# Second attention of a two-block gated cross-attention network: another order of the steps on TensorE

## The chip, the cores and the metric

The kernel runs on one core of a Trainium2 chip. The metric is the device time of one execution in microseconds, as the median of several runs.

## What is computed

The network takes 32 sequences of 128 tokens with 128 channels (x) and a context of 77 tokens with 128 channels for each sequence. It has two blocks. Each is a gated attention to the context, then a gated feed-forward that sends every token to one of eight experts. The part that matters here is the second block:

```
x = x + tanh(g_xattn[0]) * attention_0(layernorm(x), ctx)            # one head
x = x + tanh(g_ffn[0])   * experts_0(layernorm(x))                   # 8 experts and a shared one
x = x + tanh(g_xattn[1]) * attention_1(layernorm(x), ctx)            # 16 heads of 8, relative bias, no mask set
x = x + tanh(g_ffn[1])   * experts_1(layernorm(x))

def attention_1(q, ctx):
    scores = q_heads @ k_heads.T * scale + rel_bias                  # 16 heads, 128 x 77 each
    return (softmax(scores) @ v_heads).merge_heads() @ Wo + bo

def experts_1(x):                                                    # 8 maps of 128 x 128
    idx = argmax(x @ sign(tile_sigs).T)
    return (x @ W[idx] + b[idx])
```

All arithmetic on TensorE is in float32.

## The kernel before

The kernel works through stages: the first attention, the first feed-forward, and then one loop (`attend_1`) that does the second attention and the second feed-forward together, one sequence (batch) at a time. The change lies in this loop. Its first transpose on TensorE starts at 229.9 us, and it ends with the span.

Each engine has its own list of steps with a lag. `pipeline` goes through turns; in turn i it runs, in the order of the list, each step for batch i minus the step's lag. A turn thus holds steps of several batches side by side, and the order of the list is the order in which the engine issues. An engine that waits holds all that stands behind it in its list. There are 32 batches and the largest lag on TensorE is 5, so it takes 37 turns. In the first turns, parts of the first feed-forward's shared expert are mixed in (`shared`).

These are the steps on TensorE, by the line of their matmul:

- `norm_T` (L1267, lag 0), `queries` (L1271, lag 1): the normed input is transposed and projected.
- `scores(0)`, `scores(1)` (L1281 and L1285): scores of eight heads each, in products that use 32 rows of the array. VectorE adds the relative bias behind them (`bias`, L1482).
- `probs_T(0)` to `probs_T(3)` (L1295): the 16 heads' scores are kept in ten blocks of 128 columns, which are transposed 4, 1, 4 and 1 at a time. Those of the first half are already exponentials. Those of the second half come from VectorE's subtraction of the maximum (L1499); ScalarE takes the exponential when it copies them out of PSUM. The copies on ScalarE (L1400) are 512 and 128 columns wide.
- `weigh(0)` to `weigh(3)` (L1309): products of these with the values, eight matmul instructions each, for four outputs of 32 columns of the array. weigh(n) waits for ScalarE's copy of probs_T(n). weigh(0) and weigh(1) give the first half, weigh(2) and weigh(3) the second.
- `heads_T` (L1321), `mixed_T` (L1326), `project` (L1330, lag 4): the outputs are transposed, divided by the sums on VectorE (`mix`), transposed and projected. VectorE adds the residual (`residual`, L1520 to L1525).
- `norm3_T` (L1337, lag 4), `signature` (L1341, lag 5), `choice_T` (L1354, lag 5), `maps(0)` and `maps(1)` (L1349, lag 5), `picked_bias` (L1358, lag 5): the feed-forward. All of them write PSUM bank 7, one after another. VectorE stands between them: `choose` (L1532 to L1539) after the signature, `pick(0)` (L1550) after maps(0), `pick(1)` (L1553) after maps(1), `add_bias` (L1559) after picked_bias. ScalarE copies norm3_T's result (L1428) and choice_T's (L1433).

ScalarE's list has the copies in this order: norm3_T, probs_T(1), mixed_T, norm_T, probs_T(2), choice_T, probs_T(3), then the eight exponentials of the first half (L1390), the heads' copy (L1418) and the queries' (L1383).

VectorE's list is: choose, bias(0), maxima(0), residual, pick(0), bias(1), stats2 (L1470, L1473), pick(1), maxima(1), add_bias, mix, subtract.

Of the kernel before, what the change touches and what calls it, by code (L numbers as in the profile page):

```python
# [135 lines left out]
def wait(eng, sem, value):  # L136

    if isinstance(value, int) and value <= 0:
        return
    eng.wait_ge(sem, value)  # L140
# [8 lines left out]
def pipeline(eng, n, stages, ways=2, begin=None):  # L149

    first = min(lag for _, lag in stages)
    stages = [(stage, lag - first) for stage, lag in stages]
    span = max(lag for _, lag in stages)
    turns = -(-(n + span) // ways)

    for i in range(turns):
        if begin:
            begin(i)  # L160
        for u in range(ways):
            for stage, lag in stages:
                item = ways * i + u - lag
                if 0 <= item < n:
                    stage(item, (u - lag) % ways)
# [1019 lines left out]
def attend_1(nc, sb, sem, sems, bank, out, m, f, units):  # L1185
# [64 lines left out]
    def pe_program(pe):  # L1250
# [3 lines left out]
        def shared(place):  # L1254
            def stage(b, u):
                for n in range(*(PE_SHARED.get((place, b), (0, 0)) if isinstance(b, int) else (0, 0))):
                    j, part = piece(n)
                    if part < HC:
                        units["gate_up"](pe, EARLY + j, part)
                    else:  # L1260
                        units["down"](pe, EARLY + j)
            return stage
# [10 lines left out]
        def scores(half):  # L1273
            def stage(b, u):
                if half == 0:
                    pe.wait_ge(s["qs"], b + 1)
                    pe.wait_ge(s["kb"], b + 1)
                wait(pe, s["sb"], NHF * b + half)
                for i in two:
                    rows = slice(32 * (2 * half + i), 32 * (2 * half + i) + 32)  # L1280
                    nc.tensor.matmul(bS[i][:, 0:HG * SK], onesb[rows, :],  # L1281
                                     padR[rows, b:b + 1, :].to_broadcast([32, HG, SK]), start=True, stop=False)
                for i in two:
                    rows = slice(32 * (2 * half + i), 32 * (2 * half + i) + 32)
                    nc.tensor.matmul(bS[i][:, 0:HG * SK], QT[u][rows, :], KB[u][rows, :, :],  # L1285
                                     start=False, stop=True).then_inc(s["sc"], 1)
            return stage

        def probs_T(n):
            def stage(b, u):  # L1290
                half, end = divmod(n, 2)
                pe.wait_ge(s["su" if half else "ex"], b + 1)
                wait(pe, s["pTs"], N * b + n - 1)
                for i, c in enumerate(range(half * BH + end * HG, half * BH + (BH if end else HG))):
                    last = nc.tensor.transpose(bP[end][:, i * 128:i * 128 + 128], SB[u][:, c, :], ident)  # L1295
                last.then_inc(s["pT"], 1)
            return stage

        def weigh(n):
            def stage(b, u):  # L1300
                half, end = divmod(n, 2)
                pe.wait_ge(s["pTs"], N * b + n + 1)
                if n == 0:
                    pe.wait_ge(s["vp"], b + 1)
                    wait(pe, s["os"], b)
                    if isinstance(b, int) and b == 0:
                        pe.wait_ge(h["prod"], 2 * (EARLY + LATER) - 1)
                for j in range(HG):
                    last = nc.tensor.matmul(bO[32 * j:32 * j + 32, half * S:half * S + S],  # L1309
                                            VP[u][:, half, j, end, :, :].rearrange("p t r -> p (t r)"),  # L1310
                                            PT[half][:, (j + end) * S:(j + end) * S + S], start=(end == 0), stop=(end == 1))
                last.then_inc(s["pv"], 1)
            return stage
# [29 lines left out]
        def maps(k):  # L1343
            def stage(b, u):
                if k == 0:
                    pe.wait_ge(s["hTs"], b + 1)
                else:
                    pe.wait_ge(s["pk"], 2 * b + 1)
                nc.tensor.matmul(bF[:, :], xn3T[u][:, :], w2[:, k * HT:(k + 1) * HT, :], start=True, stop=True).then_inc(s["f"], 1)  # L1349
            return stage  # L1350
# [5 lines left out]
        def picked_bias(b, u):  # L1356
# [1 line left out]
            nc.tensor.matmul(bF[:, 0:128], OHT[u][:, :], b2[:, :], start=True, stop=True).then_inc(s["fb"], 1)  # L1358

        pipeline(pe, B, [  # L1360
            (signature, 5), (weigh(0), 3), (probs_T(2), 3), (weigh(1), 3), (probs_T(3), 3), (choice_T, 5),
            (project, 4), (weigh(2), 3), (maps(0), 5), (scores(1), 2), (weigh(3), 3), (maps(1), 5),
            (shared("queries"), 0), (queries, 1), (shared("T0"), 0), (probs_T(0), 2), (heads_T, 3),
            (picked_bias, 5), (shared("sc01"), 0), (scores(0), 1), (norm3_T, 4), (probs_T(1), 2),
            (mixed_T, 3), (shared("norm_T"), 0), (norm_T, 0)])
# [329 lines left out]
```

## Time and profile before

| | |
|---|---|
| median of 3 runs | 538.32 us (538.27 to 540.05) |
| the profiled execution, its own time | 539.62 us |
| its span | 537.8 us |
| TensorE matmul busy over the span | 484.3 us (90%) |
| VectorE | 383.5 us (71%) |
| ScalarE | 311.1 us (58%) |
| GpSimd | 353.2 us (66%) |

The span runs from the first to the last instruction on the chip; the time has a little more around it. A busy share is a mean over stages with different limits, and a matmul's record includes the time until the array is through with it, so that records overlap. In the profile's rows PE is TensorE, PEld its weight loads, DVE VectorE, ACT ScalarE and POOL GpSimd.

### The profile page before, as it was taken

To read this page: it belongs to the slowest core of one execution; us is meant where nothing else is said; L and a number is where in the kernel's file an instruction comes from. 1 tells how busy PE (TensorE), PEld (TensorE's weight loads), DVE (VectorE), ACT (ScalarE), POOL (GpSimd) and SP (SyncE) were. 2 spreads that over 40 slices of the span, in tenths; PEclk is the share of its full clock that TensorE was granted. 3 is DMA by queue.
4 is the path that set the end of the run, shared out by engine and by line. 5 is a ranking of instruction groups with operands and counts; after the bars stand their busy time and mean duration, and the time that the engine had idled before them with its cause. 6 is when DMAs were issued, how large, how long until landed. Compare 5 with 4: busy or idle time off the path is not lost.

```text
span 537.8 us, 12347 instructions
## 1 busy us (share of the span) xinstructions
PE 484.3 (90%) x3355; PEld 304.2 (57%) x3355; DVE 383.5 (71%) x1146; ACT 311.1 (58%) x1013; POOL 353.2 (66%) x845
## 2 busy tenths in 40 slices
PE   6868798589999999789999999999999999999863
PEld 5757687346655666565555556555555555556420
DVE  3778788548433434336999999999999999998631
ACT  3667687422245555258776766667666776766410
POOL 5574688877135555454778878788887878877421
PEclk9999897569999999959999999999999999999955
DMA  9855250022134322100000000000000000000000
GB/s 230 163 101 148 70 175 15 22 69 70 34 87 119 87 75 71 44 11 6 12 22 11 22 12 21 21 12 21 11 21 21 12 22 11 21 12 11 6 11 5
DMA packets 33924, 25.78 MB, mean 48 GB/s; under 512 B 8104, under 2 KB 31280, under 8 KB 33824
## 3 DMA queue, kind: packets, MB, share of 16 engines
q1 hardware_dynamic: 30864, 19.48, 14.6%
q0 software_dynamic: 2272, 4.67, 2.8%
q10 hardware_dynamic: 720, 0.83, 0.6%
q8 instruction: 29, 0.48, 0.4%
q14 instruction: 39, 0.32, 0.2%
HBM read 16.89 MB, written 8.39 MB: 47 GB/s over the span
## 4 chain that ended last, share of the span: by engine, by line
PE 47%; DVE 3%; issue 1%; POOL 0%; ACT 0%; POOLq 0%; DVEq 0%
PE bank L1349 13%; PE bank L1309 8%; PE bank L1295 8%; PE bank L1285 6%; PE bank L1358 2%; PE bank L1341 2%; PE bank L1281 1%; PE bank L1337 1%; PE bank L1326 1%; PE bank L1330 1%; PE bank L1271 1%; PE bank L1321 1%; PE bank L1354 1%; PE bank L1267 1%; DVE V L1550 1%
## 5 line engine op out<-in xcount | busy, mean ns | idle before, releaser
L1349 PE MATMUL bank<-w,xn3T 128*128 128x512 f32 x128 | 75.8, 676 | 2.4 <-DVE V L1550 2.0
L1390 ACT ACTIVATE wgu<-wgu,top 128x77 f32<-128x77 f32 x256 | 67.4, 347 | 15.5 <-DVE top L1492 15.5
L1400 ACT ACTIVATE PRT<-bank 128x512 f32<-128x512 f32 (+1 forms) x128 | 54.4, 426 | 29.5 <-PE bank L1295 29.5
L970 POOL DMA_INDIRECT routed<-ys,to x39 | 37.2, 953 | 48.1 <-DVE ys L1173 39.9
L1295 PE MATMUL bank<-cst,wgu 128*128 128x128 f32 x320 | 60.2, 286 | 0.4 <-ACT wgu L1390 0.2
L1482 DVE TENSOR_TENSOR wgu<-bank,biasQ 128x616 f32<-128x616 f32 x64 | 50.8, 794 | 8.6 <-PE bank L1285 7.0
L1309 PE MATMUL bank<-PRT,VP 128*32 128x128 f32 x1024 | 54.5, 285 | 0.7 <-ACT PRT L1400 0.7
L1492 DVE TENSOR_REDUCE top<-wgu 128x8 f32<-128x616 f32 x64 | 50.3, 785 | 1.1
L1285 PE MATMUL bank<-KB,QT 32*128 32x308 f32 x256 | 50.3, 434 | 0.0
L1625 POOL TENSOR_TENSOR wgu<-V 128x256 f32<-128x256 f32 x32 | 37.8, 1180 | 16.1 <-DVE V L1553 16.1
L1295 PEld LDWEIGHTS bank<-cst,wgu 128*128 128x128 f32 x320 | 37.8, 142 | 14.9 <-issue 13.4
L1168 DVE TENSOR_TENSOR hid<-actg,bank 128x256 f32<-128x256 f32 x39 | 16.4, 421 | 41.4 <-ACT actg L1077 41.4
L1026 PE MATMUL bank<-wgu,xsT 128*128 x78 | 40.7, 604 | 0.4 <-ACT xsT L1072 0.4
L833 POOL DMA_INDIRECT sorted_x<-XN,slot x32 | 33.3, 1040 | 8.5 <-issue 8.2
L1585 POOL TENSOR_TENSOR VP<-XN,cst 128x64 f32<-128x64 f32 x128 | 35.4, 308 | 0.0
L1309 PEld LDWEIGHTS bank<-PRT,VP 128*32 128x32 f32 x1024 | 20.1, 108 | 24.6 <-issue 19.1
L1604 POOL TENSOR_TENSOR x2b<-x,rows 128x128 f32<-128x128 f32 x32 | 14.5, 454 | 24.9 <-DVE x L1520 24.9
L1349 PEld LDWEIGHTS bank<-w,xn3T 128*128 128x128 f32 x128 | 19.9, 195 | 18.1 <-DVE V L1550 9.7
L1553 DVE COPY_PREDICATED V<-OH,bank 128x512 f32<-128x512 uint32 x32 | 23.5, 735 | 9.2 <-PE bank L1349 7.0
L1499 DVE TENSOR_TENSOR wgu<-wgu,top 128x616 f32<-128x616 f32 x32 | 27.0, 844 | 0.0
L1042 PE MATMUL bank<-wdn,hidT 128*128 x156 | 25.8, 288 | 1.1 <-ACT hidT L1082 1.1
L1077 ACT ACTIVATE actg<-bank 128x256 f32<-128x256 f32 x39 | 15.0, 384 | 20.2 <-PE bank L1026 20.2
(231 smaller groups left out, 1260.2 us busy)
## 6 DMA issues: line engine op xcount, KB each, us to landing
xs<-sorted_x SPq DMA_DIRECT2D x39, 64.5 KB, 1.8
wgu<-in_wgu SPq DMA_DIRECT2D x4, 512.0 KB
y<-routed SPq DMA_DIRECT2D x32, 64.0 KB, 1.8
out<-res SPq DMA_DIRECT2D x32, 64.0 KB, 1.7
ctxT<-in_ctxT SPq DMA_DIRECT2D x16, 77.0 KB, 3.2
mask<-in_mask SPq DMA_DIRECT2D x16, 77.0 KB, 3.9
wdn<-in_wdn SPq DMA_DIRECT2D x2, 512.0 KB
X<-in_x SPq DMA_DIRECT2D x1, 768.0 KB, 5.7
```

The source lines that it names most:

```text
L970: nc.gpsimd.indirect_dma_start(routed, bass.IndirectOffsetOnAxis(ap=to[:, t:t + 1], axis=0), ys[t % WAYS][:, :], None).then_inc(st_y[t % W ...
L1026: nc.tensor.matmul(bH[t % 2][:, :], xsT[t % 2][:, :], wgu[:, bass.ds(experts[t], 1), :], start=True, stop=True).then_inc(e["h"], 1)
L1285: nc.tensor.matmul(bS[i][:, 0:HG * SK], QT[u][rows, :], KB[u][rows, :, :], start=False, stop=True).then_inc(s["sc"], 1)
L1295: last = nc.tensor.transpose(bP[end][:, i * 128:i * 128 + 128], SB[u][:, c, :], ident)
L1309: last = nc.tensor.matmul(bO[32 * j:32 * j + 32, half * S:half * S + S], VP[u][:, half, j, end, :, :].rearrange("p t r -> p (t r)"), PT[ha ...
L1349: nc.tensor.matmul(bF[:, :], xn3T[u][:, :], w2[:, k * HT:(k + 1) * HT, :], start=True, stop=True).then_inc(s["f"], 1)
L1390: last = nc.scalar.activation(SC[u][:, head, :], SC[u][:, head, :], ACT.Exp, bias=top[u][:, head:head + 1])
L1400: nc.scalar.activation(PT[half][:, k], bP[end][:, 0:k.stop - k.start], ACT.Exp if half else ACT.Copy).then_inc(s["pTs"], 1)
L1482: nc.vector.tensor_tensor(half(SC[u][:, k, :]), bSS.rearrange("p c (h k) -> p c h k", h=HG), half(biasQ[:, k, :]), ALU.add).then_inc(s["sb ...
L1492: nc.vector.tensor_reduce(top[u][:, k], SC[u][:, k, :], AX.X, ALU.max, negate=(h == 0)).then_inc(s["mx" if h else "lo"], 1)
L1585: last = nc.gpsimd.tensor_tensor(VP[u][:, c, :, end, :, 0:HD], VF[:, first:first + HG, bass.ds(b, 1), :].to_broadcast([128, HG, 2, HD]), o ...
L1625: nc.gpsimd.tensor_tensor(sum2[u][:, :, :], picked[u][:, 0:2, :], picked[u][:, 2:4, :], ALU.add).then_inc(s["s2"], 1)
```

## The change

In the list of TensorE's steps, weigh(1) moves ahead of probs_T(2), project moves ahead of choice_T, and weigh(3) moves from behind scores(1) to directly behind weigh(2), ahead of maps(0). The lags stay, and so do the lists of all other engines.

```diff
         pipeline(pe, B, [
-            (signature, 5), (weigh(0), 3), (probs_T(2), 3), (weigh(1), 3), (probs_T(3), 3), (choice_T, 5),
-            (project, 4), (weigh(2), 3), (maps(0), 5), (scores(1), 2), (weigh(3), 3), (maps(1), 5),
+            (signature, 5), (weigh(0), 3), (weigh(1), 3), (probs_T(2), 3), (probs_T(3), 3), (project, 4),
+            (choice_T, 5), (weigh(2), 3), (weigh(3), 3), (maps(0), 5), (scores(1), 2), (maps(1), 5),
             (shared("queries"), 0), (queries, 1), (shared("T0"), 0), (probs_T(0), 2), (heads_T, 3),
             (picked_bias, 5), (shared("sc01"), 0), (scores(0), 1), (norm3_T, 4), (probs_T(1), 2),
             (mixed_T, 3), (shared("norm_T"), 0), (norm_T, 0)])
```

In the rows of the two programs a name on the right of the arrow is what is read: PRT and VP are the copied exponentials and the values, cst is the identity of a transpose, wgu the scores, OH the choice, AOT and wc the projection, xn3T and w (or w2) the maps. A float32 matmul is one row here and two records in the trace.

The first place is TensorE between the signature and the first maps of one turn, before:

```order
L1341 MATMUL bank<-wc,xn3T 128x8
L1309 MATMUL bank<-PRT,VP 32x128 x4
L1295 MATMUL bank<-cst,wgu 128x128 x4
L1309 MATMUL bank<-PRT,VP 32x128 x4
L1295 MATMUL bank<-cst,wgu 128x128
L1354 MATMUL bank<-cst,OH 8x128
L1330 MATMUL bank<-wc,AOT 128x128
L1309 MATMUL bank<-PRT,VP 32x128 x4
L1349 MATMUL bank<-w,xn3T 128x512
```

And the same place after:

```order
L1341 MATMUL bank<-wc,xn3T 128x8
L1309 MATMUL bank<-PRT,VP 32x128 x8
L1295 MATMUL bank<-cst,wgu 128x128 x5
L1330 MATMUL bank<-wc,AOT 128x128
L1354 MATMUL bank<-cst,OH 8x128
L1309 MATMUL bank<-PRT,VP 32x128 x8
L1349 MATMUL bank<-w,xn3T 128x512
```

Three blocks of four products with the values have become two of eight, and the second of them holds weigh(3), which stood behind the first maps.

The second place is TensorE from the first maps to the queries, before:

```order
L1349 MATMUL bank<-w,xn3T 128x512
L1281 MATMUL bank<-padR,onesb 128x308 x2
L1285 MATMUL bank<-KB,QT 128x308 x2
L1309 MATMUL bank<-PRT,VP 32x128 x4
L1349 MATMUL bank<-w,xn3T 128x512
L1271 MATMUL bank<-xn2T,wc 128x128
```

And after:

```order
L1349 MATMUL bank<-w,xn3T 128x512
L1281 MATMUL bank<-padR,onesb 128x308 x2
L1285 MATMUL bank<-KB,QT 128x308 x2
L1349 MATMUL bank<-w,xn3T 128x512
L1271 MATMUL bank<-xn2T,wc 128x128
```

The products of weigh(3) no longer stand between scores(1) and the second maps.

## Rows read from the trace of the kernel before

**Rows 1.** Three stretches: start:end, length; busy and count by engine; granted clock; DMA.

```profile
440.00:460.00 20.00, 20.00 (x171) 11.39 (x169) 18.47 (x44) 14.19 (x50) 16.05 (x45) 1.00 0.07 21
495.40:503.80 8.40, 7.69 (x64) 4.17 (x64) 7.23 (x18) 5.03 (x18) 3.68 (x9) 1.00 0.03 8
511.80:521.80 10.00, 6.54 (x13) 2.49 (x12) 3.31 (x10) 1.31 (x4) 2.85 (x8) 0.57 0.02 7
```

**Rows 2.** TensorE in order of time, one turn: start us, us, line, tiles.

```profile
444.61 0.39 PE L1341 MATMUL bank<-wc,xn3T 128*128 128x8 f32 x2
444.93 0.43 PE L1309 MATMUL bank<-PRT,VP 128*32 128x128 f32 x8
445.29 0.66 PE L1295 MATMUL bank<-cst,wgu 128*128 128x128 f32 x4
...
446.23 0.33 PE L1295 MATMUL bank<-cst,wgu 128*128 128x128 f32 x1
446.40 0.27 PE L1354 MATMUL bank<-cst,OH 128*8 128x128 f32 x1
446.50 0.39 PE L1330 MATMUL bank<-wc,AOT 128*128 128x128 f32 x2
446.82 0.43 PE L1309 MATMUL bank<-PRT,VP 128*32 128x128 f32 x8
447.18 1.12 PE L1349 MATMUL bank<-w,xn3T 128*128 128x512 f32 x2
...
448.99 0.43 PE L1309 MATMUL bank<-PRT,VP 128*32 128x128 f32 x8
449.35 1.13 PE L1349 MATMUL bank<-w,xn3T 128*128 128x512 f32 x2
...
451.31 0.37 PE L1358 MATMUL bank<-b,OHT 8*128 8x128 f32 x1
...
453.07 0.39 PE L1341 MATMUL bank<-wc,xn3T 128*128 128x8 f32 x2
```

**Rows 3.** Line L1341 over the span: ns min/median/max, first and last start.

```profile
L1341 PE MATMUL bank<-wc,xn3T x64: 256/275/381, 258.1 to 522.1; 128*128 128x8 f32 x64
```

**Rows 4.** VectorE in order of time, in the same turn.

```profile
445.70 0.40 DVE L1539 TENSOR_SCALAR OH<-am 128x8 f32<-128x8 f32 x1
...
448.25 0.18 DVE L1525 BATCH_NORM_AGGREGATE mv<-st 128x2 f32<-128x6 f32 x1
448.38 0.69 DVE L1550 TENSOR_TENSOR V<-bank,OH 128x512 f32<-128x512 f32 x1
...
450.24 0.18 DVE L1473 BATCH_NORM_AGGREGATE mv<-st 128x2 f32<-128x6 f32 x1
450.51 0.74 DVE L1553 COPY_PREDICATED V<-OH,bank 128x512 f32<-128x512 uint32 x1
...
451.84 0.35 DVE L1559 SCALAR_TENSOR_TENSOR x3b<-bank,dead,x 128x128 f32<-128x128 f32 x1
```

**Rows 5.** ScalarE in order of time, in the same turn and just before.

```profile
443.02 0.58 ACT L1400 ACTIVATE PRT<-bank 128x512 f32<-128x512 f32 x1
443.50 0.48 ACT L1406 ACTIVATE xn<-x,nb,r 128x128 f32<-128x128 f32 x1
...
445.98 0.60 ACT L1400 ACTIVATE PRT<-bank 128x512 f32<-128x512 f32 x1 [0.91 <-PE bank L1295]
446.70 0.27 ACT L1433 ACTIVATE OHT<-bank 8x128 f32<-8x128 f32 x1
446.88 0.25 ACT L1400 ACTIVATE PRT<-bank 128x128 f32<-128x128 f32 x1
```

**Rows 6.** TensorE in narrow windows: the halves of one block of products.

```profile
444.93 0.32 PE L1309 MATMUL bank<-PRT,VP 128*32 128x128 f32 x4
...
445.06 0.29 PE L1309 MATMUL bank<-PRT,VP 128*32 128x128 f32 x4
```

**Rows 7.** TensorE in the last turns: a pair of maps records.

```profile
513.93 2.08 PE L1349 MATMUL bank<-w,xn3T 128*128 128x512 f32 x2
```

## Prediction

> **What bounds the kernel now.** I read the busy times first, then the table of stretches, then the order of time of one turn on TensorE, ScalarE and VectorE. In the second attention TensorE is shown busy for all of 20 us in the stretch from 440 to 460 us, VectorE for 18.5 of them, ScalarE for 14.2 and GpSimd for 16.1, at the full clock (1.00, the 2.4 GHz level) [rows 1]. A busy TensorE is not proof that it sets the pace: its records overlap and a matmul that drains counts as busy. So I followed one turn, from the signature product at 444.61 to the next one at 453.07, which is 8.46 us [rows 2]. The 32 signatures lie between 258.1 and 522.1 us [rows 3], 8.5 apart in the mean (264.0 / 31), so this turn stands for the stage.
>
> A chain through one PSUM bank (bank 7) closes on itself once in a turn: signature, choice on VectorE, choice_T on TensorE, its copy on ScalarE, first maps, first pick on VectorE, second maps, second pick, picked bias, its addition on VectorE, third norm's transpose and its copy, and the next signature. The links that I use: the choice ends at 446.10 and choice_T starts at 446.40, though an engine's end reaches a waiting TensorE product in 0.06 (second pick ends 450.51 + 0.74 = 451.25, picked bias starts 451.31) [rows 2, 4]. The copy of the choice ends at 446.97 and the first maps start at 447.18, 0.21 later, because the third product block (weigh(2)) stands between [rows 2, 5]. The first pick ends at 449.07 and the second maps start at 449.35, 0.28 later, because weigh(3) stands between [rows 2, 4]. So TensorE's order has slack in the chain at three places. VectorE is close behind: its first pick starts 0.05 before the previous operation's end (448.25 + 0.18 = 448.43 against 448.38), as two independent operations do there, and 0.08 after the first maps end (447.18 + 1.12 = 448.30), where 0.03 is enough at the second pick (449.35 + 1.13 = 450.48, then 450.51) [rows 2, 4]. The first pick is therefore held by VectorE with 0.05 to spare on TensorE's side, and from there to the second pick both engines are within 0.2 of each other. Any delay of the first maps beyond 0.05 is a delay of VectorE too, and VectorE has no idle stretch in which to win it back.
>
> **The change, part by part.** No instruction is added or removed and VectorE, ScalarE, GpSimd and the queues keep their order. The moves are all on TensorE.
>
> (a) weigh(1) goes ahead of the third transposes (probs_T(2)), so weigh(0) and weigh(1) form one block of sixteen products. A block of eight takes 0.36 from its first start to the next group's first (444.93 to 445.29) [rows 2]. Its second group of four products starts 0.13 after the first (444.93, 445.06) [rows 6]. The longer block then takes 0.36 + 2 x 0.13 = 0.62, and probs_T(2) starts at 445.55 in place of 445.29, 0.26 later. Bounds: 0.22, if four more cost only what the busy time shows (0.43 for eight against 0.32 for four) [rows 2, 6], and 0.36, a whole second block.
>
> (b) probs_T(2), probs_T(3), project and choice_T follow without a block between. At steps of 0.11 (446.40 to 446.50, in rounded rows) and 0.16 after a block (446.23 to 446.40) [rows 2], with the transposes from 445.55: probs_T(3) 446.05, project 446.16 and 446.27, choice_T 446.38. It was at 446.40, and the choice that it waits for is done at 446.10 [rows 4]. So choice_T does not move, and project is earlier by 0.34. Who uses project's result (the residual on VectorE) comes to it only after its own earlier work, so that is worth nothing.
>
> (c) weigh(2) and weigh(3) now stand together ahead of the first maps, and this is where a wait arises. weigh(3) needs ScalarE's copy of probs_T(3), and ScalarE's own order is unchanged: exponentials of probs_T(2), copy of the choice, exponentials of probs_T(3). Working along it: probs_T(2) ends 0.66 after its start, at 446.21; ScalarE starts 0.03 later (445.95 to 445.98) and takes 0.60, so 446.24 to 446.84 [rows 2, 5]. The next operation on ScalarE starts 0.10 before a 128x512 copy ends (443.02 + 0.58 = 443.60 against 443.50), so the choice's copy starts at 446.74; choice_T ended by 446.65 and doesn't hold it. The copy of probs_T(3) follows 0.18 later (446.70 to 446.88), at 446.92, and takes 0.25, to 447.17 [rows 5]. With 0.06 for the signal weigh(3) starts at 447.23. TensorE would have been ready for it at 446.38 + 0.20 + 0.26 = 446.84 (0.20 is the step into a block, as from 446.61 to 446.82, where 446.61 is project's second product 0.11 after 446.50) [rows 2]. So TensorE stands for about 0.39, with the first maps, scores(1) and the second maps queued behind, and VectorE waiting for the first maps. They start 0.36 after weigh(3), at 447.59 in place of 447.18: **0.41 later**. The old order hid ScalarE's copies behind the first maps and scores(1), with weigh(3) only at 448.99 [rows 2]; that cover is gone.
>
> The Trainium skill (TensorE: Matmul & The Clock Gate, in the steps of a matmul) says that TensorE pulls only weight loads ahead and that matmuls stay in program order. This rule speaks against (c): by it the maps cannot pass a waiting weigh(3). If they could, the time would be that of the first rival; the trace of before has no such wait in a full turn to try it on.
>
> (d) weigh(3) no longer stands between scores(1) and the second maps. These can start 0.06 after the first pick in place of 0.28, so 0.22 is won on TensorE. VectorE lets only part of it through: the operation ahead of the second pick ends at 450.24 + 0.18 = 450.42, so the second pick can start at 450.37 at the earliest (the same 0.05 of overlap) in place of 450.51: 0.14 [rows 4]. After it everything is chained: picked bias 0.06 after the pick, the addition at 451.84 within 0.1 of both its operand and VectorE's previous work, and from there to the next signature [rows 2, 4]. I take 0.14; the ends are 0 and 0.22.
>
> **Sum.** 0.41 - 0.05 (spare at the first pick) - 0.14 = 0.22 us more in a turn. The products are in 32 turns (lag 3) and the maps in 32 (lag 5), both in 30. 30 x 0.22 = 6.6. The two first turns with products have no maps; there weigh(3)'s wait falls on scores(1) in place of the maps and the block saved stands against it, taken as zero. The last turns without products don't change. The profiled execution took 539.62 us, 537.8 of it span and 1.8 around it; by its own time the sum gives 546.2, and it lies 1.3 above the median of the runs. For the median: 538.3 + 6.6 = **544.9**. With the bounds (0.22 won and 0.04 less in the block: 0.10 in a turn; nothing won and no spare: 0.41) it is 541.3 to 550.6.
>
> **Rivals.**
>
> First, weigh(3) doesn't hold the maps, **not slower but faster**. The place is the same, the point is whether TensorE comes to weigh(3) after ScalarE's copy is done: 446.84 against 447.17. Were the copies 0.4 quicker, the first maps would start at 446.58 + 0.62 = 447.20, inside the spare, and the 0.14 of (d) would be the whole effect: 30 x 0.14 = 4.2, so 534.1. For it speaks that a block's way in costs 0.20 and not 0.11. Against it, three durations on ScalarE that are alike in every turn. The Trainium skill (TensorEngine Tiling (Array Packing), Key Properties) says that a change of tiling mode drains TensorE; the rows agree with 0.20 against 0.11. Taken as the only thing that counts, four blocks of 0.36 become two of 0.62 and two ways in of 0.09 extra go, 0.38 a turn: 538.3 - 11.4 = 526.9. Against that last time stands VectorE without idle stretches. Chance 0.11 for both together, 0.02 of it for the second.
>
> Second, it comes out even: (d) gives back what (c) takes, because VectorE's small gaps between dependent operations close up once its operands are early. That wants 0.36 won where I see 0.14 to 0.22. Time 538 to 540, chance 0.12.
>
> Third, the stall costs the clock. At the end of the span the granted clock is 0.57 in a stretch in which TensorE is busy for 6.5 of 10 us [rows 1], and a maps pair takes 2.08 at that level in place of 1.12 [rows 2, 7]. Ten turns at the low level cost at least 10 x 2 x 0.95 = 19 us: 564. Against it: a stall of 0.39 leaves TensorE busy for over 95% of a turn, and it kept 1.00 at 7.7 of 8.4 us [rows 1]. Chance 0.02.
>
> That the change doesn't do what it says has no chance: the order on TensorE shows both blocks joined.
>
> **How the numbers follow.** The forecast has 0.75. The range for 8 in 10 is 539.5 to 550.0: the forecast's own span but its extreme end, and a part of the second rival. About 0.5% of the time, 2.7 us, is what a measurement can tell from no change, so faster means under 535.6 and slower over 541.0. Faster 0.11, from the first rival. Same 0.14, from the second and the lower edge of the forecast. Slower 0.75, from the rest and the clock.
>
> **What the changed profile would show.** Turns of about 8.68 in place of 8.46, read from signature to signature; probs_T(2) about 0.9 after the signature; weigh(3) waiting for ScalarE's copy, and the first maps about 2.98 after the signature (2.57 before); VectorE idle for about 0.35 ahead of the first pick; the second maps within 0.06 of the first pick's end. A turn under 8.46 with no wait at weigh(3) would say that ScalarE's copies were not in the way; first maps that late in a turn of 8.46 would say that the chain is not what sets the pace.

## The result and the profile after

The changed kernel takes 544.25 us (543.13 to 545.64, 6 runs) against 539.16 us (537.82 to 540.65, 6 runs) of the kernel before, run beside it. The ratio is 1.0095, interval 1.0070 to 1.0121: slower by 5.1 us. The forecast was 544.9, slower, with a range of 539.5 to 550.0.

The profiled execution has a span of 543.8 us (537.8 before). First the busy times of the page, then the stretch that [rows 1] shows of before:

```profile
PE 477.1 (88%) x3355; PEld 302.7 (56%) x3355; DVE 378.3 (70%) x1146; ACT 310.6 (57%) x1013; POOL 357.8 (66%) x845
```

```profile
440.00:460.00 20.00, 19.30 (x175) 11.45 (x174) 17.70 (x45) 13.01 (x46) 16.43 (x42) 1.00 0.05 16
```

TensorE is less busy than before (477.1 against 484.3 us) and the time is longer: joined blocks take less of its time, but it now stands in every turn. The clock in this stretch is unchanged at 1.00. This is the turn on TensorE in order of time (start us, us, line), as in [rows 2]:

```profile
449.34 0.39 PE L1341 MATMUL bank<-wc,xn3T 128*128 128x8 f32 x2
449.66 0.64 PE L1309 MATMUL bank<-PRT,VP 128*32 128x128 f32 x16
450.23 0.77 PE L1295 MATMUL bank<-cst,wgu 128*128 128x128 f32 x5
450.84 0.39 PE L1330 MATMUL bank<-wc,AOT 128*128 128x128 f32 x2
451.06 0.27 PE L1354 MATMUL bank<-cst,OH 128*8 128x128 f32 x1
451.58 0.73 PE L1309 MATMUL bank<-PRT,VP 128*32 128x128 f32 x16 [0.24 <-ACT PRT L1400]
452.24 1.13 PE L1349 MATMUL bank<-w,xn3T 128*128 128x512 f32 x2
...
453.45 0.68 PE L1285 MATMUL bank<-KB,QT 32*128 32x308 f32 x4
454.15 1.12 PE L1349 MATMUL bank<-w,xn3T 128*128 128x512 f32 x2
```

The first maps start 2.90 us after the signature (452.24 - 449.34). Before it was 2.57 [rows 2]. The second product block carries a new note: it waited for ScalarE's copy (PRT, L1400). Its sixteen records take 0.73 where the first block's take 0.64, because weigh(3) inside it waits a second time. The list of waits (who waited for whom, us in total, times, longest) has it 19 times between 340 and 500 us, once in each turn, where before it was not listed:

```profile
PEld bank L1309 <- ACT PRT L1400: 9.7, 19, 0.5
```

ScalarE in the same turn, to be held against [rows 5]:

```profile
450.93 0.60 ACT L1400 ACTIVATE PRT<-bank 128x512 f32<-128x512 f32 x1 [1.12 <-PE bank L1295]
451.42 0.25 ACT L1433 ACTIVATE OHT<-bank 8x128 f32<-8x128 f32 x1
451.58 0.25 ACT L1400 ACTIVATE PRT<-bank 128x128 f32<-128x128 f32 x1
```

The copy of probs_T(2) ends at 451.53 and weigh(2) starts at 451.58; the copy of probs_T(3) ends at 451.83, and the maps follow 0.41 later. So TensorE stands twice in this block. It comes to weigh(2) 0.52 after choice_T (451.06 to 451.58), where such a step takes 0.20 without a wait (425.94 to 426.14 in the rows of one_block_noswap below): about 0.32 for the copy of probs_T(2). From its start to the maps the block takes 0.66 (451.58 to 452.24), where the first block takes 0.57 (449.66 to 450.23): 0.09 more for the copy of probs_T(3). VectorE, to be held against [rows 4]:

```profile
450.42 0.23 DVE L1539 TENSOR_SCALAR OH<-am 128x8 f32<-128x8 f32 x1
...
452.82 0.18 DVE L1525 BATCH_NORM_AGGREGATE mv<-st 128x2 f32<-128x6 f32 x1
453.40 0.69 DVE L1550 TENSOR_TENSOR V<-bank,OH 128x512 f32<-128x512 f32 x1 [0.40 <-PE bank L1349]
454.20 0.80 DVE L1482 TENSOR_TENSOR wgu<-bank,biasQ 128x616 f32<-128x616 f32 x1
...
455.31 0.18 DVE L1473 BATCH_NORM_AGGREGATE mv<-st 128x2 f32<-128x6 f32 x1
455.44 0.73 DVE L1553 COPY_PREDICATED V<-OH,bank 128x512 f32<-128x512 uint32 x1
```

VectorE, which had no idle time ahead of the first pick, now stands 0.40 there for the first maps. The second maps start 0.06 after the first pick (453.40 + 0.69 = 454.09, then 454.15), and the second pick begins 0.05 before the operation ahead of it ends (455.31 + 0.18 = 455.49), so VectorE holds it.

Taken over all turns in the middle of the stage (the median distance of signatures in the trace), a turn is 8.64 us in place of 8.46 (0.185 more, unrounded), and the first maps stand at 2.90 in place of 2.56. The first and the last signature are 269.0 apart, before 263.8: 5.2 more, the worth of 28 such turns (28 x 0.185).

### The profile page after: what moved, and what is told of

It reads as the page before. It is cut to its first block, busy times and chain, and to the rows that moved or that the text cites. A ratio compares the mean times of both kernels' runs of the same rounds, so it can differ in the third digit from the quotient of the medians.

```text
span 543.8 us, 12347 instructions
## 1 busy us (share of the span) xinstructions
PE 477.1 (88%) x3355; PEld 302.7 (56%) x3355; DVE 378.3 (70%) x1146; ACT 310.6 (57%) x1013; POOL 357.8 (66%) x845
## 4 chain that ended last, share of the span: by engine, by line
PE 50%; DVE 10%; issue 8%; ACT 5%; POOL 5%; SPq 3%; DMA 3%; DVEq 0%; POOLq 0%
PE bank L1349 8%; PE bank L1309 7%; PE bank L1285 7%; PE bank L1295 4%; DVE V L1553 4%; ACT PRT L1400 4%; PE bank L1026 3%; PE bank L1358 3%; PE bank L980 2%; DMA xs<-sorted_x 2%; PE bank L1341 2%; PE bank L981 2%; PE bank L1281 2%; PE bank L991 2%; PE bank L1042 2%
## 5 line engine op out<-in xcount | busy, mean ns | idle before, releaser
L1400 ACT ACTIVATE PRT<-bank 128x512 f32<-128x512 f32 (+1 forms) x128 | 54.3, 426 | 35.9 <-PE bank L1295 35.8
L1295 PE MATMUL bank<-cst,wgu 128*128 128x128 f32 x320 | 53.1, 281 | 0.3 <-ACT wgu L1390 0.3
L1309 PE MATMUL bank<-PRT,VP 128*32 128x128 f32 x1024 | 43.8, 282 | 8.7 <-ACT PRT L1400 8.7
L1585 POOL TENSOR_TENSOR VP<-XN,cst 128x64 f32<-128x64 f32 x128 | 51.2, 431 | 0.0
L833 POOL DMA_INDIRECT sorted_x<-XN,slot x32 | 34.4, 1074 | 8.5 <-issue 8.2
L1625 POOL TENSOR_TENSOR wgu<-V 128x256 f32<-128x256 f32 x32 | 23.8, 744 | 17.9 <-DVE V L1553 17.9
L1309 PEld LDWEIGHTS bank<-PRT,VP 128*32 128x32 f32 x1024 | 22.2, 108 | 23.1 <-ACT PRT L1400 17.9
L1550 DVE TENSOR_TENSOR V<-bank,OH 128x512 f32<-128x512 f32 x32 | 22.1, 692 | 16.7 <-PE bank L1349 16.6
L1383 ACT ACTIVATE QT<-bank,qbias,qscale 128x128 f32<-128x128 f32 x32 | 14.6, 457 | 26.4 <-PE bank L1271 26.3
L1612 POOL TENSOR_TENSOR v2e<-mv,eps 128x1 f32<-128x1 f32 x32 | 6.1, 192 | 32.6 <-DVE mv L1473 32.6
```

What stands on the lines that cost most here:

```text
L1400: nc.scalar.activation(PT[half][:, k], bP[end][:, 0:k.stop - k.start], ACT.Exp if half else ACT.Copy).then_inc(s["pTs"], 1)
L1585: last = nc.gpsimd.tensor_tensor(VP[u][:, c, :, end, :, 0:HD], VF[:, first:first + HG, bass.ds(b, 1), :].to_broadcast([128, HG, 2, HD]), o ...
```

## Experiments

The theory: TensorE stands at weigh(3) for the copy of probs_T(3), which on ScalarE comes behind that of probs_T(2) and that of the choice; the first maps behind it set the length of the turn. The rivals: the longer block that puts off probs_T(2), the place of project, TensorE's busy time as such, or that weigh(3) stands ahead of the maps at all, with its own length and without any wait. In this table "maps" is the start of the first maps after the signature and "turn" the distance of two signatures, both as medians over the middle of the stage.

| kernel | time us | ratio to before, interval | maps | turn |
|---|---|---|---|---|
| before | 539.16 | | 2.56 | 8.46 |
| changed | 544.25 | 1.0095 (1.0070 to 1.0121) | 2.90 | 8.64 |
| w3_alone | 546.17 | 1.0116 (1.0088 to 1.0145) | 2.93 | 8.67 |
| w3_stays | 539.87 | 1.0011 (0.9992 to 1.0029) | 2.59 | 8.48 |
| act_swap | 542.75 | 1.0066 (1.0044 to 1.0088) | 2.81 | 8.56 |
| no_w3 | 535.41 | 0.9924 (0.9897 to 0.9951) | 2.57 | 8.31 |
| t_first | 543.58 | 1.0123 (1.0085 to 1.0162) | 2.91 | 8.65 |
| t_first_noswap | 554.80 | 1.0311 (1.0280 to 1.0342) | 3.27 | 9.02 |
| w3_behind | 549.74 | 1.0223 (1.0187 to 1.0259) | 2.65 | 8.86 |
| one_block | 535.41 | 0.9951 (0.9936 to 0.9967) | 2.59 | 8.33 |
| one_block_noswap | 535.32 | 0.9951 (0.9927 to 0.9975) | 2.59 | 8.33 |

Each row's ratio is to the kernel before on the same chip in the same set of runs: its median was 539.45 us beside w3_alone, w3_stays, act_swap and no_w3, 538.26 beside t_first, t_first_noswap, w3_behind and one_block, and 538.51 beside one_block_noswap. The times are medians of 4 to 10 runs, of 2 for t_first_noswap. The ratios are those on record and can differ a little from the quotient of two medians: t_first has 1.0123, and 543.58 / 538.26 is 1.0099. w3_alone, no_w3 and w3_behind are edits of the kernel before; w3_stays, act_swap and both t_first are edits of the changed one.

**weigh(3) alone is moved ahead of the maps.**

```diff
-            (project, 4), (weigh(2), 3), (maps(0), 5), (scores(1), 2), (weigh(3), 3), (maps(1), 5),
+            (project, 4), (weigh(2), 3), (weigh(3), 3), (maps(0), 5), (scores(1), 2), (maps(1), 5),
```

> Kernel before, with weigh(3) moved to directly behind weigh(2) and nothing else. Theory (TensorE stands at weigh(3) for ScalarE's copy of probs_T(3), which comes behind the copy of the choice): probs_T(2) keeps its place, but choice_T still ends 2.06 us after the signature, so the choice's copy runs 2.09 to 2.36 and the copy of probs_T(3) to 2.51; weigh(3) at 2.57, first maps at 2.93 (2.56 before, 2.90 in the changed kernel), turns of 8.65 to 8.68, time 5 to 7 us over before: 544 to 546. Rival (the longer block that puts off probs_T(2) is what costs): turns of 8.30 to 8.46, time at or under that of before.

It took 546.17 us, turns 8.67. This one move costs all that the whole change costs. TensorE's turn from choice_T on, and ScalarE's copies:

```profile
434.37 0.27 PE L1354 MATMUL bank<-cst,OH 128*8 128x128 f32 x1
...
434.80 0.79 PE L1309 MATMUL bank<-PRT,VP 128*32 128x128 f32 x16
435.51 0.70 PE L1349 MATMUL bank<-w,xn3T 128*128 128x512 f32 x1
```

```profile
433.95 0.60 ACT L1400 ACTIVATE PRT<-bank 128x512 f32<-128x512 f32 x1 [0.90 <-PE bank L1295]
434.68 0.27 ACT L1433 ACTIVATE OHT<-bank 8x128 f32<-8x128 f32 x1
434.85 0.25 ACT L1400 ACTIVATE PRT<-bank 128x128 f32<-128x128 f32 x1
```

probs_T(2) kept its old place here, and its copy is done at 434.55. But the choice's copy waits for choice_T (434.37 + 0.27 = 434.64) and holds the copy of probs_T(3) to 435.10. The maps come 0.41 after that, as in the changed kernel. The maps are 0.36 later than before, and the stand is the smaller part of it: the block takes 0.71 to the maps (434.80 to 435.51) where 0.57 is a block of sixteen without a wait, so 0.14 is the stand at weigh(3), and about 0.21 (0.57 against 0.36) is the length of weigh(3) itself.

**weigh(3) put back, the rest of the change kept.**

```diff
-            (choice_T, 5), (weigh(2), 3), (weigh(3), 3), (maps(0), 5), (scores(1), 2), (maps(1), 5),
+            (choice_T, 5), (weigh(2), 3), (maps(0), 5), (scores(1), 2), (weigh(3), 3), (maps(1), 5),
```

> The changed kernel with weigh(3) put back behind scores(1); weigh(1) ahead of probs_T(2) and project ahead of choice_T remain. Theory: weigh(2) waits for the later copy of probs_T(2), starts 2.24 after the signature, first maps at 2.60, 0.04 later than before; turns of 8.46 to 8.50, time 0 to 1.5 us over before. Rival (the longer block or project's place is what costs): turns of 8.60 or more, time 5 us over before.

It took 539.87 us, a ratio that can't be told from 1, with turns of 8.48. The longer first block and project's place cost next to nothing, and they gain nothing either. TensorE does stand at weigh(2), as in the changed kernel:

```profile
429.25 0.43 PE L1309 MATMUL bank<-PRT,VP 128*32 128x128 f32 x8 [0.25 <-ACT PRT L1400]
```

That stand by itself leaves the maps at 2.59, 0.03 later than before.

**ScalarE copies probs_T(3) ahead of the choice.**

```diff
-            (probs_T(1), 2), (mixed_T, 3), (shared("xTs"), 0), (norm_T, 0), (probs_T(2), 2), (choice_T, 4),
-            (probs_T(3), 2), (exps(0), 1), (heads, 2), (shared("qs"), 0), (queries, 0), (norm3, 3)])
+            (probs_T(1), 2), (mixed_T, 3), (shared("xTs"), 0), (norm_T, 0), (probs_T(2), 2), (probs_T(3), 2),
+            (choice_T, 4), (exps(0), 1), (heads, 2), (shared("qs"), 0), (queries, 0), (norm3, 3)])
```

> The changed kernel with two steps of ScalarE's list exchanged: the copy of probs_T(3) ahead of the copy of the choice. Theory: weigh(3) can start 0.16 earlier, first maps 2.74 after the signature (2.90), turns of 8.48 (8.64), time 1 us over before, about 540. Rival (TensorE's stand has another cause than this order on ScalarE, such as the length of the products or the copy of the choice itself): first maps and turns as in the changed kernel, 544, or later because the choice's copy is later.

Half a hit. The maps moved from 2.90 to 2.81, not to 2.74, and the time to 542.75. By the times alone the two kernels can't be told apart, since the intervals of their ratios overlap; the turns can (8.56 against 8.64). The direction says that the order of the copies is part of the cause. TensorE's rows say what came next:

```profile
429.59 0.27 PE L1354 MATMUL bank<-cst,OH 128*8 128x128 f32 x1
430.11 0.64 PE L1309 MATMUL bank<-PRT,VP 128*32 128x128 f32 x16 [0.25 <-ACT PRT L1400]
430.68 0.70 PE L1349 MATMUL bank<-w,xn3T 128*128 128x512 f32 x1
```

The block runs through in 0.64 now, without the second wait inside, but it starts as late as before, behind the copy of probs_T(2). From its start the block alone needs 0.57 to the maps. So there are two stands, one at weigh(2) and one at weigh(3), and the exchange removes only the second. Set beside w3_stays, which has the same stand at weigh(2), this kernel shows what weigh(3) costs ahead of the maps without a wait of its own: the maps are 0.22 later (2.81 against 2.59) and 0.14 comes back behind them, 0.08 in a turn (8.56 against 8.48). The wait at weigh(3) adds another 0.08 (8.64). My expectation had worked from weigh(3)'s readiness and had left out that the block's own length stood just behind it.

**weigh(3) left out.** This kernel leaves out the products of weigh(3), with weigh(2) counting for both in the semaphore and two of its products on other value columns. The diff shows the list alone, not the edited lines of weigh.

```diff
-            (project, 4), (weigh(2), 3), (maps(0), 5), (scores(1), 2), (weigh(3), 3), (maps(1), 5),
+            (project, 4), (weigh(2), 3), (maps(0), 5), (scores(1), 2), (maps(1), 5),
```

> Kernel before without weigh(3): its four products are left out (and two of weigh(2)'s read other value columns, so that every sum has a positive denominator). Theory (the second pick gains 0.13 when the second maps follow the first pick at once, and VectorE lets no more through): turns of 8.32, time 4 us under before, about 535; VectorE's order is then what holds the second pick. Rival 1 (TensorE's busy time is the pace): 0.36 to 0.45 less in a turn, 526 to 528. Rival 2 (the place of weigh(3) costs nothing there): turns of 8.45, 539.

535.41 us, turns of 8.31: the whole worth of a free way from scores(1) to the second maps is 0.14 in a turn, although TensorE has a block of 0.36 less to do. The VectorE rows show why it is no more:

```profile
427.40 0.69 DVE L1550 TENSOR_TENSOR V<-bank,OH 128x512 f32<-128x512 f32 x1
...
429.30 0.18 DVE L1473 BATCH_NORM_AGGREGATE mv<-st 128x2 f32<-128x6 f32 x1
429.43 0.74 DVE L1553 COPY_PREDICATED V<-OH,bank 128x512 f32<-128x512 uint32 x1
```

The second pick starts 2.03 after the first, right behind the other operations of VectorE, and the same 2.03 stands in the changed kernel (455.44 - 453.40 = 2.04 in rounded rows). The time is 4.0 us under that of before, where the first rival of the prediction had 4.2, and it shows that rival's mechanism to be real where nothing waits ahead of the maps.

**weigh(3) behind the second maps.**

```diff
-            (project, 4), (weigh(2), 3), (maps(0), 5), (scores(1), 2), (weigh(3), 3), (maps(1), 5),
+            (project, 4), (weigh(2), 3), (maps(0), 5), (scores(1), 2), (maps(1), 5), (weigh(3), 3),
```

> Kernel before with weigh(3) put behind the second maps in place of ahead of them, nothing else. Theory: second maps 0.06 after the first pick, second pick 0.09 to 0.13 earlier, but the block of 0.36 and its way in then stand ahead of the queries and the picked bias, which starts about 0.2 after it could; turns of 8.50 to 8.57, time 2 to 3 us over before. Rival (TensorE has room there): turns of 8.31 to 8.33 as without weigh(3), 535.

The direction was right and the size was not: turns of 8.86, 549.74 us. The picked bias starts 0.52 after the second pick's end (median of the stage) where I had expected 0.2. These rows show TensorE from weigh(3), behind the second maps, to the picked bias:

```profile
438.83 0.42 PE L1309 MATMUL bank<-PRT,VP 128*32 128x128 f32 x8
439.19 0.49 PE L1271 MATMUL bank<-xn2T,wc 128*128 128x128 f32 x2
439.51 0.60 PE L1295 MATMUL bank<-cst,wgu 128*128 128x128 f32 x4
...
440.26 0.37 PE L1358 MATMUL bank<-b,OHT 8*128 8x128 f32 x1
```

Besides the block's 0.36 and its way in, the queries behind it take 0.32 to the next start where they took 0.22 without a block in front (450.31 to 450.53 in the kernel before). TensorE has no room at this place.

**Transposes first.** If the copies are late, their transposes can go ahead of the products.

```diff
-            (signature, 5), (weigh(0), 3), (weigh(1), 3), (probs_T(2), 3), (probs_T(3), 3), (project, 4),
+            (signature, 5), (probs_T(2), 3), (probs_T(3), 3), (weigh(0), 3), (weigh(1), 3), (project, 4),
```

The rest is as in the changed kernel; t_first has ScalarE's exchange of act_swap, t_first_noswap has not.

> The changed kernel with both transposes put ahead of weigh(0), and the copy of probs_T(3) ahead of the choice's copy on ScalarE. Theory: transposes 0.40 to 1.11 us after the signature, copies to 1.79, weigh(0) and weigh(1) meanwhile, project and choice_T from 1.62, weigh(2) and weigh(3) from 2.04 without a wait, first maps at 2.61; turns of 8.36, time 3 us under before, about 536.5. Rival as for the kernel with one block.

> The same as t_first with ScalarE's list left as it was (the choice's copy ahead of that of probs_T(3)). Theory: choice_T ends 2.11 us after the signature, its copy at 2.42, the copy of probs_T(3) at 2.55, weigh(3) at 2.61, first maps at 2.96; turns of 8.71, slower than the changed kernel although the transposes are 0.5 earlier; time 546. Rival (the late transposes are what holds weigh(3)): as t_first, 536.5.

Both missed in absolute size, t_first by its sign: the maps stand at 2.91, the time is 543.58. These are TensorE's rows of t_first:

```profile
428.66 0.39 PE L1341 MATMUL bank<-wc,xn3T 128*128 128x8 f32 x2
429.20 0.77 PE L1295 MATMUL bank<-cst,wgu 128*128 128x128 f32 x5 [0.15 <-DVE wgu L1499]
429.90 0.64 PE L1309 MATMUL bank<-PRT,VP 128*32 128x128 f32 x16
...
430.80 0.27 PE L1354 MATMUL bank<-cst,OH 128*8 128x128 f32 x1
431.00 0.64 PE L1309 MATMUL bank<-PRT,VP 128*32 128x128 f32 x16
431.58 0.70 PE L1349 MATMUL bank<-w,xn3T 128*128 128x512 f32 x1
```

The transposes wait for VectorE's subtraction (L1499) and start 0.54 after the signature, not 0.40, and the way into and out of the first block, which I had left out of the sum, puts off choice_T to 2.14. No product waits here: this order is simply too much work between signature and maps. The difference between the two kernels is what the theory had said: without the exchange on ScalarE the maps come 0.36 later (3.27 against 2.91; expected 2.96 against 2.61), although probs_T(3) is transposed early in both. That is the choice's copy in front of the copy of probs_T(3), by itself, as the rows of t_first_noswap show:

```profile
440.70 0.25 ACT L1400 ACTIVATE PRT<-bank 128x128 f32<-128x128 f32 x1
```

```profile
441.00 0.43 PE L1309 MATMUL bank<-PRT,VP 128*32 128x128 f32 x8 [0.16 <-ACT PRT L1400]
```

**One block.** choice_T goes as early as VectorE allows, and all products stand together behind it, as one block of 32 records (a product is two records), so that they cover the copies. The diff is against the kernel before; one_block has ScalarE's exchange of act_swap too, one_block_noswap has not.

```diff
-            (signature, 5), (weigh(0), 3), (probs_T(2), 3), (weigh(1), 3), (probs_T(3), 3), (choice_T, 5),
-            (project, 4), (weigh(2), 3), (maps(0), 5), (scores(1), 2), (weigh(3), 3), (maps(1), 5),
+            (signature, 5), (probs_T(2), 3), (probs_T(3), 3), (project, 4), (choice_T, 5), (weigh(0), 3),
+            (weigh(1), 3), (weigh(2), 3), (weigh(3), 3), (maps(0), 5), (scores(1), 2), (maps(1), 5),
```

> Another order on TensorE and ScalarE made from the theory: after the signature both transposes (probs_T(2), probs_T(3)), project and choice_T, then all four product blocks as one of thirty-two, then the first maps; on ScalarE the copy of probs_T(3) ahead of the choice's copy. Theory: the copies of the transposes (1.04 to 1.79 us after the signature) and of the choice (to about 2.0) are done while the earlier products run, nothing waits at weigh(3), and the first maps start at about 2.56; the second maps follow the first pick at once. Turns of 8.31 to 8.36 (before 8.46), time 3 to 4.5 us under before: 535 to 536.5. Rival (what costs is that weigh(3) stands ahead of the maps at all, not its wait): turns of 8.55 or more, time over before.

> The order with one block of thirty-two products on TensorE, with ScalarE's list as in the kernel before (the choice's copy ahead of that of probs_T(3)). Theory: choice_T ends 1.64 us after the signature, so the choice's copy runs 1.73 to 2.00 and the copy of probs_T(3) to 2.16; TensorE comes to weigh(3) at about 2.23 and does not wait; first maps at 2.59, turns of 8.33, time 535.4, as with ScalarE's lists exchanged. Rival (the exchange on ScalarE is what made that order faster): first maps 0.1 or more later, turns of 8.43 or more, time 538 or more.

Both as expected: 535.41 and 535.32 us, turns of 8.33, ratio 0.9951 to before (0.9936 to 0.9967 and 0.9927 to 0.9975). This order beats both kernels, and ScalarE's list can stay as it was. Here weigh(3) stands ahead of the maps too, and they are at 2.59: where TensorE doesn't wait for a copy, it has room for weigh(3) there. What the order wins over before is the 0.14 behind the maps. TensorE and ScalarE of one_block_noswap:

```profile
424.56 0.39 PE L1341 MATMUL bank<-wc,xn3T 128*128 128x8 f32 x2
425.10 0.76 PE L1295 MATMUL bank<-cst,wgu 128*128 128x128 f32 x5
...
425.94 0.27 PE L1354 MATMUL bank<-cst,OH 128*8 128x128 f32 x1
426.14 1.08 PE L1309 MATMUL bank<-PRT,VP 128*32 128x128 f32 x32
427.15 1.13 PE L1349 MATMUL bank<-w,xn3T 128*128 128x512 f32 x2
```

```profile
425.79 0.60 ACT L1400 ACTIVATE PRT<-bank 128x512 f32<-128x512 f32 x1 [0.76 <-PE bank L1295]
426.29 0.25 ACT L1433 ACTIVATE OHT<-bank 8x128 f32<-8x128 f32 x1
426.44 0.25 ACT L1400 ACTIVATE PRT<-bank 128x128 f32<-128x128 f32 x1
```

The copy of probs_T(3) is done at 426.69. A block of eight more adds 0.21 to 0.22 (0.36, 0.57 and 1.01 to the next start for one, two and four), so weigh(3) is due at 426.14 + 3 x 0.22 = 426.80 and doesn't wait. One block of thirty-two costs one way in and one way out, and its first half is the cover that weigh(3) had lost in the change.

## Why the prediction was right

Read down the table, turn minus maps is 5.74 to 5.75 in eight kernels: changed, w3_alone, act_swap, no_w3, both t_first and both one_block. It is 5.89 to 5.90 in before and in w3_stays, where weigh(3) stands between scores(1) and the second maps. So the prediction's split of the turn, a late first maps at full price and a fixed 0.14 back from the freed second maps, holds for the maps anywhere from 2.57 to 3.27. w3_behind (6.21) is apart, since there a block stands behind the second maps.

By its own steps:

- (a), the longer block: 0.62 to probs_T(2) was forecast, 0.57 measured (449.66 to 450.23). The term was mis-sized: each further group of four records cost 0.11, as the bound by the busy time had said, not the 0.13 between the starts of the first two fours.
- (b): choice_T at 1.72 after the signature (1.77 forecast, 1.79 before). That project's place is worth nothing agrees with w3_stays, which leaves out only weigh(3)'s move, though it was not tried alone.
- (c), the wait: the copy of probs_T(3) does set when the maps start, by the chain that was forecast. The delay of the maps was forecast too large, 0.41 where 0.33 was measured (medians of 2.897 and 2.564). Of the 0.08, 0.05 is (a). The rest is smaller steps on ScalarE: the copy of probs_T(3) starts 0.16 behind the choice's, not 0.18.
- (c), the place of the stand: the prediction put all 0.39 at weigh(3), with TensorE ready for it at 446.84. It left out that weigh(2) waits too: by its own times TensorE is there at 446.58, and the copy of probs_T(2) ends at 446.84. Measured is about 0.32 at weigh(2) and 0.09 at weigh(3). The sum didn't suffer, since the wait at weigh(3) still ends last (by 0.07 in the prediction's times: 446.84 + 0.06 + 0.26 = 447.16 against 447.23). act_swap's expectation did, and so would anyone who mended only the copy of probs_T(3).
- The sentence that the order rule "speaks against (c)" is the wrong way round: that matmuls keep their order is what (c) needs. In the changed kernel the maps start behind the waiting block, and the wait stands in every turn.
- The 0.05 of spare at the first pick was no gain. The pick does start sooner after the maps (453.37 to 453.40 = 0.03, before 0.08), but VectorE's next operation, bias(1), waits for scores(1), which follows the maps at a fixed distance (453.45 - 452.24 = 1.21, before 448.38 - 447.18 = 1.20). bias(1) starts 0.07 after scores(1) ends (453.45 + 0.68 = 454.13, then 454.20), before 0.08 (448.38 + 0.68 = 449.06, then 449.14). I had measured it from the pick. This step failed, by 0.05 in a turn.
- (d): 0.14 forecast. From the first maps to the second pick it was 3.33 [rows 2, 4] and is 3.20 (452.24 to 455.44): 0.13, or 0.14 by the medians over all turns. VectorE's order sets that limit, as the prediction had it, and no_w3 shows the same limit with no wait anywhere.
- The sum: 0.33 - 0.14 is 0.19 in a turn where 0.22 was forecast. Thirty turns at 0.185 are 5.6; 5.1 was measured between the medians and 5.2 between the signatures. That the sum came so close is in part luck: the errors went in opposite directions, the block too long and the spare counted as a gain.

These rows of the kernel before have the end of scores(1) and the start of bias(1):

```profile
448.38 0.68 PE L1285 MATMUL bank<-KB,QT 32*128 32x308 f32 x4
```

```profile
449.14 0.80 DVE L1482 TENSOR_TENSOR wgu<-bank,biasQ 128x616 f32<-128x616 f32 x1
```

The rivals. The first (no wait) fell by the rows, since the block waits in every turn, and it is the right account of no_w3 and of both one_block. Its second form, TensorE's drains as the whole matter (526.9), fell with no_w3, where TensorE loses a whole block and only 0.14 comes back. The second (it comes out even) fell by the interval. The third fell too: the clock stayed at 1.00 between 440 and 460 us.

## What to carry to other kernels

Joining products of one kind saves ways in and out of the array's tiling, but the last of the joined products brings its own length and its own producer's wait to the front of whatever stands behind the block; ask of each moved step which engine's queue delivers its operand, and what that engine has ahead of it. In a loop where each engine runs a fixed order, find the one chain that closes on itself, and price a move by what it does to that chain: here a turn's length was the first maps' place plus a constant. Cover for a late operand can be made of steps that are ready anyway: here one block with the ready half in front had the joined block's saving without its wait.

## What the runs showed of the hardware

Products with 32 columns in four places of the array start 0.007 us apart in the trace's records, and the next four start 0.11 to 0.13 after the first of them; the next operation on the whole array starts 0.20 after the last of them. A joined block of 8, 16 or 32 records took 0.36, 0.57 and 1.01 to the next start.

The last operation of the choice on VectorE (L1539) took 0.40 in the kernel before and 0.23 in the changed one, with the same operands. GpSimd's first sum (L1625) took 1.29 and then 0.73. In the kernel before, L1539 starts 0.08 behind GpSimd's second sum (L1627, 445.62 to 446.07) and ends 0.03 after it; in the changed kernel it starts 0.15 ahead of that sum (450.42 and 450.57). In the kernel before GpSimd's sum runs while VectorE subtracts:

```profile
444.13 0.83 DVE L1499 TENSOR_TENSOR wgu<-wgu,top 128x616 f32<-128x616 f32 x1
444.25 1.29 POOL L1625 TENSOR_TENSOR wgu<-V 128x256 f32<-128x256 f32 x1
```

and in the changed kernel the values' product (L1585) runs there and the sum comes after it:

```profile
456.75 1.70 POOL L1585 TENSOR_TENSOR VP<-XN,cst 128x64 f32<-128x64 f32 x4
458.41 0.72 POOL L1625 TENSOR_TENSOR wgu<-V 128x256 f32<-128x256 f32 x1
```

In the kernel before the four of L1585 took 1.07 (451.68 to 452.75) and the subtraction began only at 452.59. The Trainium skill (SBUF — State Buffer, Who interferes with whom) says that a VectorE instruction with two SBUF inputs contends with a GpSimd instruction that reads SBUF, and that the order of issue decides which of them blocks. The rows agree, with 0.6 us for the GpSimd operation that starts just behind the subtraction. VectorE may lose as well: the subtraction, 0.79 to 0.83 in most kernels, takes 0.96 in act_swap, both t_first and one_block_noswap, and 1.18 in w3_behind (medians). All this was seen beside the experiments and not tried by itself. VectorE's 0.17 bought no time in the changed kernel, since choice_T stood 0.40 behind it. In one_block_noswap, where L1539 takes 0.23 too, choice_T starts 0.06 behind it (425.88 to 425.94), so part of that order's gain may rest on it; no run separates the two.
